# Attention weights of a two-layer cross-attention kernel: head sums by token tile, row-wise squares of x

## The reference

```
q = rmsnorm(x, gamma_q) @ Wq.T ; k, v = rmsnorm(ctx, gamma_kv) @ Wk.T, @ Wv.T
scores = q.k / sqrt(16) per head ; mask = |key position - idx| <= 1
w = square(relu(scores)) where mask, else 0
out = (w / max(sum(w), 1e-6)) @ v ; x1 = x + out @ Wo.T
```

## Time and profile before

| | us |
|---|---|
| median of 3 runs (lowest to highest) | 351.77 (351.51 to 351.79) |
| the profiled execution, its own time | 351.55 |
| its span (first to last instruction) | 349.7 |
| around the span | 1.85 |
| PE busy | 327.5 (94%) |
| DVE busy | 307.4 (88%) |
| ACT busy | 242.6 (69%) |
| POOL busy | 174.2 (50%) |

### The profile page before, as it was taken

The page is one execution under the profiler, slowest core; times in us unless marked ns, Lnnn a source line. Parts: engine busy times, 40 slices in busy tenths (PEclk is TensorE's granted clock), DMA queues, the critical chain, the costliest instruction groups (busy, mean ns, idle before and its releaser), DMA issues.

```text
span 349.7 us, 5560 instructions
## 1 busy us (share of the span) xinstructions
PE 327.5 (94%) x1908; PEld 236.8 (68%) x1908; DVE 307.4 (88%) x486; ACT 242.6 (69%) x491; POOL 174.2 (50%) x202
## 2 busy tenths in 40 slices
PE   2989998999999999999999999999999999999980
PEld 1564676868676768686777767676868686767750
DVE  0789597799999999999999999999999999999766
ACT  3799434276959595959595968687786868685752
POOL 3815020023838393847474746474756656444514
PEclk9999999999999999999999999999999999999995
DMA  7957714812233232414141414141413232010103
GB/s 238 354 169 191 218 60 112 226 53 87 76 108 103 77 123 67 145 60 151 60 151 60 150 63 149 62 149 62 147 63 130 82 121 90 0 62 0 62 0 121
DMA packets 22347, 38.48 MB, mean 110 GB/s; under 512 B 2160, under 2 KB 8816, under 8 KB 22320
## 3 DMA queue, kind: packets, MB, share of 16 engines
q1 hardware_dynamic: 19344, 30.01, 27.1%
q0 software_dynamic: 2016, 7.34, 6.1%
q10 hardware_dynamic: 960, 0.79, 0.7%
HBM read 17.29 MB, written 8.39 MB: 73 GB/s over the span
## 4 chain that ended last, share of the span: by engine, by line
PE 76%; DVE 9%; ACT 5%; issue 4%; POOL 2%; DMA 1%; SPq 1%; ACTq 0%; POOLq 0%
PE ps L481 11%; PE ps L482 11%; PE ps L483 11%; PE ps L560 7%; PE ps L532 7%; PE ps L526 5%; PE ps L610 4%; PE ps L641 4%; PE ps L726 4%; PE ps L717 4%; PE ps L615 2%; PE ps L513 2%; DVE qkp L1240 1%; DMA x_ring<-xT 1%; DVE ps L1251 1%
## 5 line engine op out<-in xcount | busy, mean ns | idle before, releaser
L370 POOL TENSOR_TENSOR x_lo<-x_ring,x_hi 128x1024 fp32r<-128x1024 f32 x16 | 38.4, 2398 | 38.8 <-ACT x_hi L972 38.8
L1240 DVE TENSOR_TENSOR qkp<-ps,bufs 128x1024 f32<-128x1024 f32 x48 | 55.8, 1214 | 0.9 <-PE ps L526 0.8
L1048 ACT ACTIVATE xp_hi<-bufs 128x512 fp32r<-128x512 f32 x28 | 17.7, 633 | 45.5 <-DVE bufs L1320 45.5
L410 POOL TENSOR_TENSOR bufs<-bufs,lng_twice 128x1024 f32<-128x1024 f32 x14 | 33.7, 2406 | 27.1 <-ACT bufs L1010 25.0
L383 POOL TENSOR_TENSOR mean_gap<-stats 128x4 f32<-128x4 f32 x14 | 2.8, 198 | 71.7 <-DVE stats L1309 65.0
L1251 DVE TENSOR_TENSOR ps<-ps,wn 128x1024 f32<-128x1024 f32 x31 | 37.9, 1224 | 0.0
L412 POOL TENSOR_TENSOR bufs<-bufs,lnb_row 128x1024 f32<-128x1024 f32 x14 | 33.3, 2380 | 1.1
L560 PE MATMUL ps<-qkp,cst 128*32 128x512 f32 x192 | 30.7, 598 | 0.4 <-DVE qkp L1240 0.4
L560 PE MATMUL ps<-bufs,cst 128*32 128x512 f32 x64 | 30.5, 598 | 0.0
L976 ACT ACTIVATE bufs<-ps 128x512 f32<-128x512 f32 x32 | 19.2, 602 | 14.1 <-PE ps L483 14.0
L481 PE MATMUL ps<-x_hi,wh_q 128*128 128x512 f32 x64 | 26.8, 418 | 0.0
(11 more groups left out here) (248 smaller groups left out, 927.5 us busy)
## 6 DMA issues: line engine op xcount, KB each, us to landing
x_ring<-xT SPq DMA_DIRECT2D x16, 512.0 KB, 3.5
out<-bufs POOLq DMA_DIRECT2D x14, 512.0 KB, 3.4
idx_ring<-idx SPq DMA_DIRECT2D x16, 256.0 KB, 3.9
wkv_lo<-kv SPq DMA_DIRECT2D x32, 126.0 KB
kvs<-kv SPq DMA_DIRECT2D x30, 126.0 KB
vfd<-bufs SPq DMA_DIRECT2D x8, 256.0 KB, 3.9
qkp<-ctxT SPq DMA_DIRECT2D x2, 512.0 KB, 7.3
bufs<-ctx SPq DMA_DIRECT2D x2, 512.0 KB, 8.7
```

What stands on the lines that cost most here:

```text
L370: G.tensor_tensor(x_lo[:, :, :], x_ring[:, e % RING, :, :], f32_view(x_hi[:, :, :]), ALU.subtract).then_inc(xl_ready, 2)
L410: G.tensor_tensor(zo, zn, lng_twice[:, :].unsqueeze(1).broadcast_to([P, TT, D]), ALU.mult).then_inc(zg_ready, 1)
L1240: V.tensor_tensor(qk[:, s, :, :], ps[:, bank0:bank0 + 2, :], q0, ALU.mult).then_inc(qk_ready, 1)
```

## The change

The quarters of bank 0 now belong to token tiles in place of shifts. Each of the eight matmuls takes 128 tokens of all three shifts, 384 moving columns in three pieces, and writes 384 columns of its quarter. The squares of x leave PE: the ReLU covers 384 columns and has no bias, and `s_sb` is transposed in three blocks, one for each shift. For the squares, SP loads x a second time, not transposed (`load_rows`, 512 KB a batch, into the buffer that `xsq` had), and ACT squares it in four operations of 128x256 that each also sum along the row into `floor`. DVE adds the epsilon and takes the maximum in one operation, from `floor`. In the start, `load_rows(0)` is put behind the second context load; in each step, behind the shifted copies, with a wait for the previous batch's squares. Semaphore declarations, the host's array list, and the same edits in the tail are left out below.

```diff
@@ -13,15 +13,16 @@
 EPS_RMS = 1.1920929e-07
 EPS_DEN = 1e-06
 LN_EPS = 1e-05
+FLOOR_SCALE = (16.0 * EPS_DEN / D) ** 0.5
 CT = B * K // P
 RING = 3
-C_ID, C_SEL, C_POS, C_EPS, C_END = 0, 128, 224, 225, 226
+C_ID, C_SEL, C_POS, C_END = 0, 128, 192, 193
 CENTRE, UP, DOWN = range(SHIFTS)
-def xattn_pair(nc: bass.Bass, xT, ctx, ctxT, idx, vectors, wq0T, wk0T, wv0T, wo0T,
+def xattn_pair(nc: bass.Bass, xT, x, ctx, ctxT, idx, vectors, wq0T, wk0T, wv0T, wo0T,
                wq1, wk1, wv1, wf1, bf1, ln_g, ln_b, consts, out):
     f32 = mybir.dt.float32
     f32r = mybir.dt.float32r
@@ -41,9 +42,8 @@
         cst = sb("cst", [P, C_END])
         ident = cst[:, C_ID:C_ID + P]
-        sum_sel = cst[:, C_SEL:C_SEL + 96].rearrange("p (g c) -> p g c", g=3)
+        sum_sel = cst[:, C_SEL:C_SEL + 64].rearrange("p (g c) -> p g c", g=DC)
         pos = cst[:, C_POS:C_POS + 1]
-        den_eps = cst[:, C_EPS:C_EPS + 1]
         vec = sb("vec", [P, 5, DC])
         bf_row = sb("bf_row", [P, D])
         lng_row = sb("lng_row", [P, D])
@@ -98,7 +98,9 @@
         nbias = sb("nbias", [P, TT])
         bufs = sb("bufs", [P, 8, DC * T])
-        xsq, q0, xpT, q1T = (bufs[:, n, :].rearrange("p (c t) -> p c t", c=DC) for n in (0, 3, 4, 5))
+        q0, xpT, q1T = (bufs[:, n, :].rearrange("p (c t) -> p c t", c=DC) for n in (3, 4, 5))
+        x_rows = bufs[:, 0, :].rearrange("p (j d) -> p j d", j=TT)
+        floor = sb("floor", [P, 2, TT])
         zn, zo = (bufs[:, n, :].rearrange("p (j d) -> p j d", j=TT) for n in (6, 7))
@@ -121,15 +123,15 @@
         ps = es.enter_context(nc.psum_tensor("ps", [P, 8, 512], f32))
-        by_token = ps[:, 0, :].rearrange("p (j r) -> p j r", j=TT)
-        w = by_token[:, :, 0:32 * SHIFTS].rearrange("p j (s h) -> p s j h", h=32)[:, :, :, 0:H]
-        den_floor = by_token[:, :, 96:97]
+        by_shift = ps[:, 0, 0:SHIFTS * P]
+        w = by_shift.rearrange("p (s j h) -> p s j h", s=SHIFTS, h=32)[:, :, :, 0:H]
         sc_rows = ps[:, 4, 2 * P:4 * P].rearrange("p (j n) -> p j n", n=K)
         ex = ps[:, 4, 0:2 * P].rearrange("p (j n) -> p j n", n=K)
         vec_in, cst_in, wk1_in, wkv_in, wq0_in, wv1_in, wf1_in, w1_in, ln_in, x_in, idx_in = map(sem, (
             "vec_in", "cst_in", "wk1_in", "wkv_in", "wq0_in", "wv1_in", "wf1_in", "w1_in", "ln_in", "x_in", "idx_in"))
+        rows_in = sem("rows_in")
         ctxT_in = [sem("ctxT_in0"), sem("ctxT_in1")]
         ctx_in = [sem("ctx_in0"), sem("ctx_in1")]
         half_set, cms_done, cmean_done, crs_done = map(sem, ("half_set", "cms_done", "cmean_done", "crs_done"))
...
@@ -256,6 +258,11 @@
                 sp.dma_start(x_ring[:, i % RING, :, :], xT[i].rearrange("(c p) t -> p c t", p=P)).then_inc(x_in, 16)
                 sp.dma_start(idx_ring[:, i % RING, :], idx[i].partition_broadcast(P)).then_inc(idx_in, 16)
+            def load_rows(i):
+                if i > 0:
+                    sp.wait_ge(floor_ready, TT * i)
+                sp.dma_start(x_rows, x[i].rearrange("(j p) d -> p j d", p=P)).then_inc(rows_in, 16)
+
             def cross(t):
                 sp.wait_ge(kv_hi_done, 2 * t + 2)
@@ -291,6 +298,7 @@
             sp.dma_start(idx_ring[:, 0, :], idx[0].partition_broadcast(P)).then_inc(idx_in, 16)
             context_columns(1)
             context_rows(1)
+            load_rows(0)
             weight(raw["v1"], wv1, wv1_in)
             weight(wf_raw[:, :, :], wf1, wf1_in)
             sp.dma_start(bf_row[:, :], bf1.partition_broadcast(P)).then_inc(wf1_in, 16)
@@ -334,6 +342,8 @@
                     load(e)
                 if e is not None and e >= 2:
                     shifted(e)
+                if e is not None:
+                    load_rows(e)
             steps(step)
             for m, h in FIN_ORDER:
@@ -554,11 +564,10 @@
             def head_sums(a):
                 pe.wait_ge(qk_ready, 3 * a + 3)
-                pe.wait_ge(xsq_ready, a + 1)
                 for g in range(DC):
-                    for s in range(SHIFTS + 1):
-                        i = mm(ps[32 * s:32 * s + 32, 0, :], sum_sel[:, g if s < SHIFTS else 2, :],
-                               qk[:, s, g, :] if s < SHIFTS else xsq[:, g, :], start=(g == 0), stop=(g == DC - 1))
+                    for j in range(TT):
+                        i = mm(ps[32 * j:32 * j + 32, 0, 0:SHIFTS * P].rearrange("p (s t) -> p s t", s=SHIFTS), sum_sel[:, g, :],
+                               qk[:, :, g, j * P:(j + 1) * P], start=(g == 0), stop=(g == DC - 1))
                 i.then_inc(s_mm, 1)
@@ -611,8 +620,8 @@
                         i.then_inc(o_mm, 1)
                 if f is not None:
                     pe.wait_ge(s_cp, f + 1)
-                    for j in range(TT):
-                        i = nc.tensor.transpose(ps[:, 0, j * P:(j + 1) * P], s_sb[:, j * P:(j + 1) * P], ident)
+                    for s in range(SHIFTS):
+                        i = nc.tensor.transpose(ps[:, 0, s * P:(s + 1) * P], s_sb[:, s * P:(s + 1) * P], ident)
                     i.then_inc(sT_mm, 1)
                 if f == 0:
                     keys1(1, 1)
...
@@ -976,9 +985,12 @@
                 A(q0[:, g, :], ps[:, Q0_BANKS[g], :], ACT.Copy).then_inc(q0_cp, 1)
             def square_x(a):
-                if a > 0:
-                    act.wait_ge(s_mm, a)
-                A(xsq, x_ring[:, a % RING, :, :], ACT.Square).then_inc(xsq_ready, 1)
+                act.wait_ge(rows_in, 16 * a + 16)
+                if a > 1:
+                    act.wait_ge(dcl_ready, a - 1)
+                for j in range(TT):
+                    A(x_rows[:, j, :], x_rows[:, j, :], ACT.Square, scale=FLOOR_SCALE,
+                      accum_out=floor[:, a % 2, j:j + 1]).then_inc(floor_ready, 1)
             split_context(0)
             context_squares(0)
@@ -1018,7 +1030,7 @@
                           accum_out=ssum[:, j:j + 1]).then_inc(ex_ready, 1)
                 if f is not None:
                     act.wait_ge(s_mm, f + 1)
-                    A(s_sb[:, :], ps[:, 0, :], ACT.Relu, bias=den_eps).then_inc(s_cp, 1)
+                    A(s_sb[:, 0:SHIFTS * P], by_shift, ACT.Relu).then_inc(s_cp, 1)
                 if f == 0:
                     copy_keys1(1, 0)
                 if b is not None:
@@ -1028,7 +1040,7 @@
                         A(o_hi[:, g, :], ps[:, TURN_BANKS[g], :], ACT.Copy).then_inc(oh_ready, 1)
                 if f is not None:
                     act.wait_ge(sT_mm, f + 1)
-                    by_row = w.rearrange("p s j h -> p j s h")
+                    by_row = w.rearrange("p s j h -> p (s j) h")
                     A(by_row, by_row, ACT.Square).then_inc(w_ready, 1)
                 if f == 0:
                     copy_keys1(1, 1)
...
@@ -1294,7 +1306,9 @@
                     dve.wait_ge(w_ready, f + 1)
                     V.tensor_reduce(den[:, :, :], w.rearrange("p s j h -> p j h s"), AX.X, ALU.add).then_inc(den_ready, 1)
                     dve.wait_ge(den_ready, f + 1)
-                    V.tensor_tensor(dcl[:, :, :], den[:, :, :], den_floor.broadcast_to([P, TT, H]), ALU.max).then_inc(dcl_ready, 1)
+                    dve.wait_ge(floor_ready, TT * f + TT)
+                    V.scalar_tensor_tensor(dcl[:, :, :], floor[:, f % 2, :].unsqueeze(2).broadcast_to([P, TT, H]), 16.0 * EPS_DEN * EPS_RMS,
+                                           den[:, :, :], ALU.add, ALU.max).then_inc(dcl_ready, 1)
                     dve.wait_ge(dcl_ready, f + 1)
                     V.reciprocal(rden[:, :, :], dcl[:, :, :]).then_inc(rden_ready, 1)
                     dve.wait_ge(rden_ready, f + 1)
...
@@ -1557,9 +1573,7 @@
     c[r, C_ID + r] = 1.0
     for g in range(DC):
         c[r, C_SEL + 32 * g + HPH * g + r // HD] = 1.0
-    c[:, C_SEL + 64] = 16.0 * EPS_DEN / D
     c[:, C_POS] = r % K
-    c[96, C_EPS] = 16.0 * EPS_DEN * EPS_RMS
     return c
@@ -1572,7 +1586,7 @@
     ctx = a["ctx_1024"].reshape(B * K, D)
     arrays = {
-        "xT": a["x"].transpose(0, 2, 1), "ctx": ctx, "ctxT": ctx.T, "idx": a["itok_BxS_0_255"],
+        "xT": a["x"].transpose(0, 2, 1), "x": a["x"], "ctx": ctx, "ctxT": ctx.T, "idx": a["itok_BxS_0_255"],
         "vectors": np.stack([a[n].reshape(DC, P).T for n in ("L0_xattn_gamma_q", "L0_xattn_gamma_kv", "L1_xattn_bq",
                                                              "L1_xattn_bk", "L1_xattn_bv")], axis=1),
         "wq0T": a["L0_xattn_Wq"].T, "wk0T": a["L0_xattn_Wk"].T, "wv0T": a["L0_xattn_Wv"].T, "wo0T": a["L0_xattn_Wo"].T,
```

More of the change, by code:

```diff
@@ L142, in xattn_pair @@
         kv_first = sem("kv_first")
-        onehot_ready, xsq_ready, xh_ready, xl_ready = map(sem, ("onehot_ready", "xsq_ready", "xh_ready", "xl_ready"))
+        onehot_ready, floor_ready, xh_ready, xl_ready = map(sem, ("onehot_ready", "floor_ready", "xh_ready", "xl_ready"))
         q0_mm, q0_cp, kg_mm, qk_ready, s_mm, s_cp, sT_mm, w_ready = map(sem, (
@@ L1372, in last_weights @@
                 dve.wait_ge(den_ready, LAST + 1)
```

(4 more changed lines are left out.)

## The result

The changed kernel took **360.59 us** (median of 4 runs, 356.56 to 362.07) against 351.72 us of the kernel before beside it: a ratio of 1.0215, with a 95% interval of 1.0122 to 1.0308. (The ratios leave out runs more than 1.5% above the fastest of their kernel, here the one of 362.07 us; the medians count them.) It is slower by 1.2 to 3.1%, which leaves open whether by more than 2%, and far outside the forecast of 350.2 to 353.8. A second series of the same kernel gave 356.46 us (354.41 to 359.14, ratio 1.0133, 1.0082 to 1.0185, experiment x12). The profiled execution took 359.35 us with a span of 357.6; before, the span was 349.7.

The account below looks back on a forecast made before the run. The prediction took a loop over PE and DVE as the bound. From 351.77 us, transposes (-1.5), the shorter ReLU (-0.1) and a stall in the start (+2.0) gave 352.2 us, range 350.2 to 353.8.

Parts of the forecast that it names:

- The loop over two engines: Regular step: PE and DVE alternate in a loop setting the period, 18.17 us before and 18.06 after; forecast chance 0.46.
- Head sums, 0 on the path: Head sums on PE shrink by 0.44 us a step, all absorbed by the wait ahead of the transposes: 0.
- PE is the bound: Rival, regular steps: PE sets the pace, so its savings of 0.55 us a step count, capped by DVE; 348.2 us, chance 0.14.
- Three transposes, -1.5 us: PE transposes of `s_sb` inside the loop: three for four saves 0.11 us in each of 14 steps.
- No penalty for three pieces: Head sums: a moving operand read in three pieces of 128 columns costs nothing; the opposing rival had chance 0.03.
- Squares on ACT, 0: ACT in regular steps: four squares add 0.6 us, covered by 2.71 us of idle time ahead of L1048.
- The loads, 0 in regular steps: SP's second load of x, 512 KB a batch, lands before ACT needs it in regular steps: cost 0.
- `load_rows(0)` at 0: Start: the first row load, among the first loads, costs 0, with 0.5 us as the upper end.
- The stall, +2.0 us with ends of +0.9 and +3.4: Step 2: ACT waits for batch 1's rows ahead of two copies PE needs, delaying the path once by 2.0 us.
- The landing: Start: batch 1's rows, issued at 40.6 us, land at 45.1, with ends of 44.0 and 46.5.
- the stall is longer: Rival, `square_x(1)` on ACT: rows land at 45.4 us or later, giving 352.5 us and more; chance 0.30.
- the fit cited in the prediction: Skill's transfer price, 2.0 us plus bytes over 436 GB/s: 3.2 us for 512 KB, landing 43.8, stall 0.7 us.

Follow-up runs that it names:

- x8: x1 plus four more 128-column matmuls in each group of head sums, into unused columns, so PE streams as many columns as before the change: 349.50 us, ratio 0.9926.
- x1: Changed kernel with the first squares of x moved behind the copies and the split of x, in step f == 0 only: 349.48 us, ratio 0.9927.
- x9: x1 with a fourth transpose in each step again, repeating the first block into unused columns: 351.23 us, ratio 0.9978.
- x4: Changed kernel with only the first of the 16 row loads; all batches square the rows of batch 0: 349.45 us, ratio 0.9933.
- x2: Changed kernel with `load_rows(0)` moved from the first loads to behind the last weights: 357.35 us, ratio 1.0133.
- x10: Changed kernel with POOL's first x_lo waiting until DVE has made the query weights: 356.80 us, ratio 1.0138.
- x7: x2 plus 20 matmuls into a free bank, result unread, while PE would idle in the stall: 355.30 us, ratio 1.0103.
- x13: x1 and x10 together, late squares plus POOL's wait: 349.25 us, ratio 0.9924.
- x3: Changed kernel with the edits of both x1 and x2: 349.43 us, ratio 0.9912.
- x6: Changed kernel, squares in their old place, with batch 1's row load issued right behind `load(2)`: 349.64 us, ratio 0.9939.
- x11: x2 with `load_rows(1)` issued ahead of the broadcast rows of gamma and beta: 354.18 us, ratio 0.9987, median between two clusters of runs.

## Why the prediction was wrong

Taken in the order of its steps.

- *The loop over two engines*: right. L619 is released by L1290 in all 14 waits, and the period is 18.05 us (forecast 18.06). Two of its signs were off in size. The idle time of PE's weight load ahead of L619 grew to 1.08 us, not 1.3. And of DVE's two small waits on PE the one of 0.13 us went (L1315 ends at 161.46, L1323 starts at 161.49), while the 0.26 us ahead of the second L1334, forecast at 0.15, stayed.
- *Head sums, 0 on the path*: right. Groups are 0.33 us apart, and padded back to their old length (x8) they cost nothing. "PE is the bound" would have had x8 some 6 us slower than x1.
- *Three transposes, -1.5 us*: right, a little low in size; x9 measured 1.75.
- *No penalty for three pieces*: right. The rule of the Trainium skill ("PSUM — Partial Sum Buffer", section "Specifications (TRN2)") that the prediction weighed would have made the head sums longer; this trace shows 1.50 us for 16 of them with their pipelined end, where there were 1.85. So it doesn't hold for a reading operand in three pieces of 128 columns.
- *Squares on ACT, 0*: right in size (0.40 us apiece, a wait of 2.07 us left ahead of L1060; forecast 0.42 and 2.1).
- *The loads, 0 in regular steps*: right (x4). So was `load_rows(0)` at 0 (x2), as far as 0.7 us can be told.
- *The stall, +2.0 us with ends of +0.9 and +3.4*: this step failed. Place, cause and path were right: the wait at 41 us, then squares, copies, PE's picks, L619. Its size was wrong, for three reasons.
  1. **The landing.** The prediction took 4.5 us from issue to landing, with 5.9 us as the upper end, worked out from transfers of x in regular steps and from one broadcast. It was 7.2 us in x12, 7.6 in x10, 7.9 in x2, 7.7 in x7 and x13. PE went on at 51.02 in place of 46.13: +4.9 us, not +2.0.
  2. **The clock, left out.** The prediction said that nothing on the path has slack and carried the 2.0 us through unchanged. Behind 4.86 us of idle time PE ran at 0.53 over 51 to 56 us, and L619 came at 61.63 in place of 54.42: +7.2 us, that is 2.3 more; x7 puts it at 2.5.
  3. **A late start**, in the first profile alone: the row load was issued at 44.52, 3.9 us later than the 40.6 of the forecast, which made +9.7 us of it although the landing itself took 6.1. DVE's 2.72 us are a part of it at most, since x3 and x8 issued theirs 2.6 and 2.1 us later than 40.6 without them; what all three share is PE's idle time of 1.85 or 1.86 us ahead of L491 and the lower clock behind it. Whether a late start also stands behind the other runs of that series was not measured.

With the measured terms the sum closes. For x12: +7.2 at L619 of step 3, less 0.12 for 11 steps, 1.3, is +5.9 at the L619 eleven steps on, where 263.12 - 257.26 = +5.9 is shown; the span is +5.3, so two more steps and the tail give back 0.6. For the first profile: +9.7 and +8.4 (265.67 - 257.26) at the same two places, and +7.9 in the span. Without the stall, x1 and x13 have -2.2 and -2.6 us, where the prediction had -1.6. In the profile of x1 the last L619 starts at 291.93 in place of 293.60, -1.7 us and nearly all of it from the steps, and the span is shorter by 2.0: 0.3 more come behind that L619, of which 0.1 was foreseen, for the ReLU. What the rest is, I haven't followed.

Of the rivals, "the stall is longer" was the mechanism that happened, at a chance of 0.30 and with an end of 353.6 us that was too near. That end came from a landing at 46.5, for which no row stood: the nearest row by circumstances, the row of beta, the last thing in the same queue in the same microseconds, took 4.2 us for 128 KB, when transfers of 512 KB took 3.5 elsewhere. That was a sign that transfers in this stretch are slow, and the prediction averaged it away.

**What stays open.** Why the rows take 5 to 9 us in the start: 9.1 when issued at 34.0 (x6), 7.2 to 7.9 at 40.6 to 40.9, 7.1 at 42.7 (x8), 7.7 at 43.2 (x3), 6.1 at 44.5, 5.0 at 43.2 ahead of the broadcasts (x11), and 4.8 as the median of all 16. Why the start is late in some executions and not in others, with the meeting or without it. How often POOL and DVE meet: two profiles, of the changed kernel and of x11, show it. Why POOL's `crs` is early in these was not tried.

## What to carry to other kernels

A new wait on an engine that works in order has to be followed in the first iterations by itself: list what stands behind it there, and if the waiting work isn't urgent, put it behind what is (x1 moved four squares and turned +1.3 to +2.2% into -0.7%). Price a transfer in a loaded start by the transfers of that same stretch, not by the median of the steady state, and where a stall leaves TensorE idle for about 5 us, add what its half clock costs afterwards, here half as much again. And a saving on the busiest engine counts only where nothing else releases its next instruction: 0.44 us a step of head sums were worth nothing, 0.12 us of transposes 1.75 us of the 2.2.

## What the hardware showed unexpectedly

- *TensorE's clock.* Granted clock 0.50 to 0.53 over 51 to 56 us behind 4.9 to 6.0 us without matmuls; 1.00 in the same window where 20 idle-time matmuls were put in. Worth 2.5 us at L619 and 2.5 us between the two profiled executions. In x11, behind 3.84 us without matmuls, the same window has 0.66, and PE's first two matmuls take the 0.73 us of full clock (1.22 in x2): there the clock fell only after PE had resumed.
- *Transfers.* The same 512 KB took 3.4 us (x_ring), 4.8 (rows, median) and 7.2 to 9.1 us in the start. With two broadcasts ahead in the queue they took 7.7 us (x3), without them 5.0 (x11), both issued at 43.2. While the rows of x12 were on their way, the 16 DMA engines weren't full. The DMA share by half microsecond from 30 to 50 us (the 22nd digit begins at 40.5):

```profile
DMA  0019839895999999986555552336898656542200
```

  The Trainium skill ("DMA: Bandwidth & Descriptors", section "Latency and other measured facts") has 0.2 us for an access to HBM on average and 2 us at high load. It calls this access the main part of the fixed 2 us that the fit cited in the prediction already holds. So the page's estimate stays at about 3.2 us, far short of the 7.2 shown, and no run here separates the two parts.
- *DVE beside POOL.* The second operation of the pair wh_q, 128x256 from SBUF to SBUF, took 2.46 us beside x_lo on POOL and 0.35 us alone:

```profile
L1222 DVE TENSOR_SCALAR wh_q<-vfd,vec x2: 347/1404/2462, 13.6 to 13.9; 128x256 fp32r<-128x256 f32 x2
```

  The columns before the first semicolon are the shortest, the median and the longest in ns. It ended with POOL's operation (16.3 and 16.2 us). The Trainium skill ("GPSIMD Engine Reference", section "1. Specifications") says that GpSimd shares its SBUF interfaces with VectorE and contends with some of its instructions; this trace agrees, with seven times the duration.
